# GpSimd's gathers in two graph aggregations: the wait before each step's eight gathers moves from the preceding step's gathers to those of the step two back

## The chip, the cores and the metric

One core of a Trainium2 chip runs the whole program. A core has TensorE (PE in the profile, its weight loads PEld), VectorE (DVE), ScalarE (ACT), GpSimd (POOL) and SyncE (SP), each with its own instruction stream, and 16 DMA engines. The engines meet only at semaphores. The metric is the device time in microseconds (us) of one execution. The kernel before has a median of 7060.26 us over 3 runs (7059.98 to 7061.63).

## The reference, cut to what matters

The program is a graph network of two layers on 6250 nodes with 256 features and 200000 edges `src` to `dst`. In each layer an attention aggregation over the edges is added to a dense branch, and a mixture of experts follows. The aggregation is the part that the change touches (layer 0, per head; layer 1 has the same form with 4 x 64 columns):

```
e   = leaky_relu(s[row, head] + d[col, head], 0.2)
ex  = exp(e - m[row])
den = segment_sum(ex, row, num_segments=N)
out = segment_sum((ex / den[row])[:, None] * hW[col], row, num_segments=N)
```

So for every edge a row of a table (`hW` and the scores `d`) is fetched by `col`, scaled by a weight, and summed into the row of the node that the edge belongs to.

## The kernel before, in words

`stage_sort` sorts the edges; they lie in 1616 tiles of 128 edges. `stage_aggregate` (called once for each layer by `aggregate_passes`) walks over them in 202 steps of 8 tiles (`KT`), four steps to a turn (`STEP_RING`). Layer 0 gathers rows of 68 numbers, layer 1 rows of 260. A step goes through the engines like this:

- ScalarE copies the 8 columns of indices of a step four ahead into `st_idx` (L904).
- GpSimd issues 8 indirect DMAs, one for each tile, that gather 128 rows of the table into one of the four slots of `got` (L876). This is `gather`, and its waits are what the change touches. It waits for the indices (`idx_staged`), from the second turn on for `scaled` up to the step four back (which last read the slot it now writes), and for `gathered` of the preceding step. `gathered[r]` counts the first seven gathers of a step; the eighth has a semaphore of its own, `last_in[r]`.
- SyncE loads the list of target rows, broadcast over the partitions, into `spread` (L893).
- VectorE makes a one-hot matrix `hot` (L975) and its transposed form `hot_t` in BF16 (L982). When both `gathered` and `last_in` of a step say that it has landed, it works out the exponents (L993 to L1004; L993 is the first instruction that stands behind that wait).
- ScalarE takes the exponentials (L909, L912), VectorE scales the gathered rows with them into `weighted` (L1016).
- TensorE gets the scores of a later step (L937) and sums `weighted` into blocks of 128 nodes with `hot` as the weights (L952), in a low and a high half; VectorE adds the sums to `acc` (L1024).

Each engine's order is written out by hand. In one step VectorE goes: scale step i, add the high half of step i-1, `hot` of step i+1, `hot_t` of step i+2, exponents of step i+1, add the low half of step i. Between these a "guest", the layer's dense branch, has its turn: `BallMix` in layer 0 (one tile of 128 nodes in four steps), `GateMix` in layer 1 (one tile in two steps, first "keys" in 100 steps, then "out"). The guests use TensorE, VectorE, ScalarE and SyncE, never GpSimd. TensorE's guest work stands between the scores and the high half of a step.

The DMAs of GpSimd elsewhere in the program (in the experts of layer 0, L1933 and L1939) have a wait and a `nop` ahead of each of them, but are written out without a loop.

The order in which GpSimd gathers: the first turn stands alone, then `Fori` loops over the turns, then the last turn.

Of the kernel before, what the change touches and what calls it, by code (L numbers as in the profile page):

```python
# [26 lines left out]
STEP_RING = 4  # L27
# [743 lines left out]
def stage_aggregate(nc, g, tag, table, width, shared, rows, row_list, acc, top, guest):  # L771
# [10 lines left out]
    with stage(nc) as own:  # L782
# [49 lines left out]
        def steps_of(last):  # L832
            return range(ENDING if last else STEP_RING)
# [30 lines left out]
        @block.gpsimd  # L864
        def _(pool):
            def gather(turn, r, first):
                j = turn * STEP_RING + r
                pool.wait_ge(idx_staged, j + 1)
                if not first:
                    pool.wait_ge(scaled, j - (STEP_RING - 1))  # L870
                if not first or r > 0:
                    t, q = (turn, r - 1) if r else (turn - 1, STEP_RING - 1)
                    pool.wait_ge(gathered[q], t * (16 * (KT - 1)) + 16 * (KT - 1))
                pool.nop(nofuse=True)
                for k in range(KT):
                    pool.indirect_dma_start(got[:, r, k, :], None, table,  # L876
                                            bass.IndirectOffsetOnAxis(ap=st_idx[:, r, k:k + 1], axis=0))\
                        .then_inc(gathered[r] if k < KT - 1 else last_in[r], 16)
            for r in range(STEP_RING):
                gather(0, r, True)  # L880
            with pool.Fori(1, TURNS - 1) as turn:
                for r in range(STEP_RING):
                    gather(turn, r, False)
            for r in steps_of(True):
                gather(TURNS - 1, r, False)
# [2287 lines left out]
```

## Time and profile before

| | us |
|---|---|
| median of 3 runs | 7060.26 |
| the profiled execution, its own time | 7063.9 |
| span of the profiled execution (first to last instruction) | 7062.1 |
| aggregation of layer 0, first gather to its end, from the span's start | 495 to 2741 |
| aggregation of layer 1, the same | 3581 to 5875 |
| busy over the span: PE, DVE, POOL, ACT | 5095.9, 4389.3, 3469.1, 1783.8 |
| mean granted TensorE clock, share of full speed | 0.83 |

The two aggregations are 4540 us of the span, nearly two thirds. A group of instructions in the profile is a line of the kernel, an engine, an operation and the buffers that it writes and reads, with its count, its busy time, the mean length of one in ns, and the idle time of the engine just ahead of it, by what ended that idle time ("issue": nothing that the profile shows). In a timeline each line starts with the start and the length in us, and ends with the idle time ahead of it in brackets. For a DMA that GpSimd issues the length is the time that the issuing takes; the data land later.

### The profile page before, as it was taken

How to read it: one execution, taken by the hardware profiler on the slowest of the kernel's cores; microseconds unless marked ns; L12 is line 12 of the kernel's file. 1: busy time of each engine (PE TensorE's matmuls, PEld its weight loads, DVE VectorE, ACT ScalarE, POOL GpSimd, SP SyncE). 2: the span in 40 equal slices, each digit the busy share in tenths (PEclk: the TensorE clock that was granted, in tenths of full speed). 3: DMA queues.
4: the chain of work that ended last, by engine and by line, in shares of the span. 5: the costliest groups of instructions: out<-in, count | busy, mean ns of one | idle time of the engine just before them, and what ended most of it. 6: DMA issues, size and time to landing. Idle time of an engine off the chain costs nothing. (4 is left out here: it accounts for less than half of the span.)

```text
span 7062.1 us, 90296 instructions
## 1 busy us (share of the span) xinstructions
PE 5095.9 (72%) x21196; PEld 3660.6 (52%) x21197; DVE 4389.3 (62%) x8953; ACT 1783.8 (25%) x4856; POOL 3469.1 (49%) x3669
## 2 busy tenths in 40 slices
PE   1446666666666664699766666667777777999999
PEld 1445555555555552466534444445555555666666
DVE  8987777777777778722566655556666667333333
ACT  7322222222222222222310000001111113433332
POOL 0126767666767766144146666666666664000000
PEclk8668888888888886799878887877777777999999
DMA  1022222222222222322444444444444444000001
GB/s 55 22 44 51 52 52 52 52 51 52 52 52 52 52 51 58 116 64 64 145 135 124 125 123 123 123 124 130 130 132 132 132 131 114 5 5 4 9 4 36
DMA packets 380644, 534.45 MB, mean 76 GB/s; under 512 B 119264, under 2 KB 240119, under 8 KB 380407
## 3 DMA queue, kind: packets, MB, share of 16 engines
q0 software_dynamic: 139648, 299.92, 17.8%
q1 hardware_dynamic: 240886, 233.29, 11.2%
q8 instruction: 43, 0.70, 0.0%
q14 instruction: 67, 0.54, 0.0%
HBM read 475.96 MB, written 56.96 MB: 75 GB/s over the span
## 5 line engine op out<-in xcount | busy, mean ns | idle before, releaser
L876 POOL DMA_INDIRECT got<-table,st_idx x3232 | 3092.9, 957 | 1453.5 <-issue 1004.8
L952 PE MATMUL ps_sum<-weighted,hot 128*128 128x260 f32 x6464 | 1861.2, 447 | 143.2 <-DVE acc L1024 139.0
L952 PEld LDWEIGHTS ps_sum<-weighted,hot 128*128 128x128 f32 x6464 | 1403.1, 229 | 563.0 <-DVE acc L1024 228.8
L1024 DVE TENSOR_TENSOR acc<-acc,ps_sum 128x260 f32 x1664 | 707.1, 425 | 890.3 <-PE ps_sum L952 750.0
L937 PE MATMUL ps_score<-score_split,hot_t 128*128 x3232 | 250.1, 188 | 1294.7 <-DVE z L1004 1267.5
L937 PEld LDWEIGHTS ps_score<-score_split,hot_t 128*128 128x128 bf16 x3232 | 196.8, 103 | 1471.7 <-issue 1456.7
L1016 DVE TENSOR_TENSOR weighted<-got,ps_weight 128x2048 f32<-128x2048 f32 x404 | 921.5, 2281 | 4.3 <-ACT weighted L912 0.8
L909 ACT ACTIVATE ps_weight<-z 128x32 f32<-128x32 f32 x404 | 81.2, 201 | 2969.8 <-DVE z L1004 2969.8
L3058 DVE SCALAR_TENSOR_TENSOR x_res<-ps_yf,comb,x_res 128x256 f32 x392 | 189.7, 484 | 638.0 <-PE ps_yf L2966 638.0
L975 DVE TENSOR_TENSOR hot<-ps_score,row_loc 128x1024 f32<-128x1024 f32 x404 | 492.1, 1218 | 3.5
L993 DVE TENSOR_REDUCE row_score<-ps_score 128x64 f32<-128x192 f32 (+1 forms) x404 | 163.3, 404 | 520.3 <-DMA got<-table,st_idx 518.9
L2946 PE MATMUL ps_hf<-acc,ws_f 128*128 (+2 forms) x896 | 348.2, 542 | 6.0 <-ACTq L2993 6.0
L2966 PE MATMUL ps_yf<-ws_f,h2t 128*128 128x256 f32 x1568 | 347.7, 379 | 0.8 <-ACT h2t L3006 0.8
L2946 PE MATMUL ps_hf<-h1t,ws_f 128*128 128x384 f32 (+1 forms) x896 | 346.0, 539 | 0.8 <-ACT h1t L3006 0.8
L2966 PEld LDWEIGHTS ps_yf<-ws_f,h2t 128*128 128x128 f32 x1568 | 297.8, 190 | 53.6 <-ACT h2t L3006 1.4
L3006 ACT ACTIVATE h2t<-ps_hf,own_scale 128x512 f32<-128x512 f32 x224 | 162.3, 725 | 507.9 <-PE ps_hf L2946 507.9
L2946 PEld LDWEIGHTS ps_hf<-acc,ws_f 128*128 128x128 f32 x896 | 171.1, 191 | 173.6 <-issue 114.8
L2946 PEld LDWEIGHTS ps_hf<-h1t,ws_f 128*128 128x128 f32 x896 | 170.2, 190 | 156.0 <-issue 107.1
L263 POOL TENSOR_TENSOR shifted<-xs,pivot 128x256 f32<-128x256 f32 x49 | 43.1, 880 | 382.4 <-DVE pivot L401 230.5
L1283 PE MATMUL ps_mix<-mix_xin,wq 128*128 128x128 f32 x1176 | 227.5, 379 | 0.4
L1283 PEld LDWEIGHTS ps_mix<-mix_xin,wq 128*128 128x128 f32 x1176 | 217.7, 289 | 3.7
L1939 POOL DMA_INDIRECT y_rows<-y_e,slot_home x108 | 106.6, 987 | 209.6 <-DVE y_e L2030 205.0
(533 smaller groups left out, 7558.3 us busy)
## 6 DMA issues: line engine op xcount, KB each, us to landing
spread<-row_list SPq DMA_DIRECT2D x404, 256.0 KB
got<-table,st_idx POOLq DMA_INDIRECT x3232, 2.8
gate_xin<-ball_rows SPq DMA_DIRECT2D x98, 128.0 KB
got_y_e<-y_rows SPq DMA_DIRECT2D x10, 896.0 KB
table<-row_e SPq DMA_DIRECT2D x50, 130.0 KB, 2.6
ball_rows<-xt SPq DMA_DIRECT2D x10, 640.0 KB, 4.7
mix_xin<-ball_rows SPq DMA_DIRECT2D x49, 128.0 KB
xn_rows<-xs_m SPq DMA_DIRECT2D x49, 128.0 KB, 1.7
```

Source lines behind the costliest of these rows:

```text
L876: pool.indirect_dma_start(got[:, r, k, :], None, table, bass.IndirectOffsetOnAxis(ap=st_idx[:, r, k:k + 1], axis=0))\
L937: last = nc.tensor.matmul(scores[:, k, :], hot_t[:, r % 2, k, :], split[:, :, :, :].rearrange("p t a c -> p (t a c)")[:, ds(b * SP, SP)], ...
L952: last = nc.tensor.matmul(ps_g[:, p % 2, 0:AW], hot[:, r % 2, k, :], weighted[:, r % 2, k, :], start=(k == n * p), stop=(k == n * p + n - 1))
L975: nc.vector.tensor_tensor(hot[:, r % 2, :, :], count_to.unsqueeze(1).to_broadcast([P, KT, P]), g.row_loc[:, ds(i * KT, KT)].unsqueeze(2).t ...
L993: link(nc.vector.tensor_reduce(row_score[:, :, :], scores.rearrange("p k (a c) -> p k c a", a=PARTS), AX.X, ALU.add))
L1016: nc.vector.tensor_tensor(out, v, w, ALU.mult).then_inc(scaled, 1)
L1024: nc.vector.tensor_tensor(acc[:, ds(b * AW, AW)], acc[:, ds(b * AW, AW)], ps_g[:, p % 2, 0:AW], ALU.add).then_inc(added, 1)
L1283: last = nc.tensor.matmul(bank[:, m * P:(m + 1) * P], self.mix.wq[:, c, (m0 + m) * P:(m0 + m + 1) * P], self.xin[:, c, :], start=(c == 0), ...
L2946: last = nc.tensor.matmul(ps_h[:, j, 0:HALVES[hf][1]], ws[:, par, l, c, f * P:(f + 1) * P], rhs(c, hf), start=(c == 0), stop=(c == 1))
L2966: last = nc.tensor.matmul(ps_y[:, k % 4, 0:D], h2[:, c, k * P:(k + 1) * P], ws[:, par, 2, c, :], start=(c == 0), stop=(c == 1))
L3006: nc.scalar.activation(h[:, f, at:at + n], ps_h[:, j, 0:n], ACT.Relu, bias=own_s[:, par, 1, l, f:f + 1], scale=own_s[:, par, 0, l, f:f + 1])\
L3058: nc.vector.scalar_tensor_tensor(xr, ps_y[:, k % 4, 0:D], comb[:, ds(t * 8 + pair * 2 + par, 1)], xr, ALU.mult, ALU.add).then_inc(y_used, 1)
```

## The change

In `gather`, the index of the awaited `gathered` semaphore goes from r-1 to r-2 of the ring of four (with the turn before where that is negative), and in the first turn step 1 has no such wait any more. All else is the same: the number of instructions on every engine but for that first-turn wait, the ring of four slots, the other two waits, what VectorE waits for before it reads a slot.

```
@@ -868,8 +868,8 @@
                 pool.wait_ge(idx_staged, j + 1)
                 if not first:
                     pool.wait_ge(scaled, j - (STEP_RING - 1))
-                if not first or r > 0:
-                    t, q = (turn, r - 1) if r else (turn - 1, STEP_RING - 1)
+                if not first or r > 1:
+                    t, q = (turn, r - 2) if r > 1 else (turn - 1, STEP_RING + r - 2)
                     pool.wait_ge(gathered[q], t * (16 * (KT - 1)) + 16 * (KT - 1))
                 pool.nop(nofuse=True)
                 for k in range(KT):
```

## Rows read from the trace of the kernel before

**Rows 1.** Stretches: layer 0, layer 1 keys, layer 1 out; busy us by engine.

```profile
core 0: us, PE busy (x) PEld busy (x) DVE busy (x) ACT busy (x) POOL busy (x), PEclk, DMA share, GB/s
495.00:2741.00 2246.00, 1501.48 (x7470) 1223.38 (x7470) 1648.96 (x2828) 594.55 (x2023) 1559.58 (x1616) 0.83 0.25 52
3581.00:4727.00 1146.00, 758.81 (x2904) 492.33 (x2904) 691.20 (x1321) 78.81 (x404) 768.90 (x810) 0.80 0.46 125
4727.00:5875.00 1148.00, 860.46 (x3156) 621.88 (x3156) 722.69 (x1431) 216.22 (x544) 764.42 (x806) 0.75 0.47 128
```

**Rows 2.** Timeline of POOL in layer 0, the end of one step and the next's start.

```profile
1808.63 1.21 POOL L876 DMA_INDIRECT got<-table,st_idx  x1 [0.30 <-issue]
1810.14 0.95 POOL L876 DMA_INDIRECT got<-table,st_idx  x1 [0.30 <-issue]
1812.23 0.94 POOL L876 DMA_INDIRECT got<-table,st_idx  x1 [1.14 <-DMA got<-table,st_idx]
1813.48 1.05 POOL L876 DMA_INDIRECT got<-table,st_idx  x1 [0.30 <-issue]
```

**Rows 3.** Timeline of POOL in layer 1, the first gather of a step.

```profile
4542.34 0.94 POOL L876 DMA_INDIRECT got<-table,st_idx  x1 [1.28 <-DMA got<-table,st_idx]
```

**Rows 4.** Line L876 in layer 0 (495 to 2741): us from issue to landing.

```profile
DMA to landing us min/median/max: 2.3/2.5/4.1
```

**Rows 5.** Line L876 in layer 1 (3581 to 5875): us from issue to landing.

```profile
DMA to landing us min/median/max: 2.7/2.8/4.7
```

**Rows 6.** Groups by line, POOL, layer 0 (495 to 2741).

```profile
L876 POOL DMA_INDIRECT got<-table,st_idx x1616 | 1559.6, 965 | 694.8 <-issue 494.8 <-DMA got<-table,st_idx 165.5 <-DVE weighted L1016 17.4
```

**Rows 7.** The same, layer 1 keys (3581 to 4727).

```profile
L876 POOL DMA_INDIRECT got<-table,st_idx x810 | 768.9, 949 | 388.6 <-issue 255.9 <-DMA got<-table,st_idx 117.5 <-ACT st_idx L904 14.5
```

**Rows 8.** The same, layer 1 out (4727 to 5875).

```profile
L876 POOL DMA_INDIRECT got<-table,st_idx x806 | 764.4, 948 | 370.2 <-issue 254.0 <-DMA got<-table,st_idx 115.6 <-ACT st_idx L904 0.6
```

**Rows 9.** Timeline of POOL: the stages' first gathers, a first and a last stall.

```profile
495.42 1.44 POOL L876 DMA_INDIRECT got<-table,st_idx  x1 [16.38 <-ACT st_idx L904]
...
653.26 0.95 POOL L876 DMA_INDIRECT got<-table,st_idx  x1 [1.68 <-issue]
...
3581.77 1.19 POOL L876 DMA_INDIRECT got<-table,st_idx  x1 [12.35 <-ACT st_idx L904]
...
5853.10 0.94 POOL L876 DMA_INDIRECT got<-table,st_idx  x1 [1.67 <-issue]
```

**Rows 10.** Waits of POOL over the span, for the gathers of the experts: total, times, longest.

```profile
POOL xin_e L1933 <- issue: 31.7, 104, 0.3
```

**Rows 11.** Timeline of POOL: the shortest idle time ahead of a step.

```profile
2134.30 0.94 POOL L876 DMA_INDIRECT got<-table,st_idx  x1 [0.72 <-DMA got<-table,st_idx]
```

**Rows 12.** Timeline, all engines: the scaling of one step, and the slot's next gather.

```profile
1826.42 2.28 DVE L1016 TENSOR_TENSOR weighted<-got,ps_weight 128x2048 f32<-128x2048 f32 x1
...
1829.69 0.22 ACT L904 COPY st_idx<-col_idx 128x8 int32 x1
...
1855.69 0.94 POOL L876 DMA_INDIRECT got<-table,st_idx  x1 [1.15 <-DMA got<-table,st_idx]
```

**Rows 13.** Groups by line, DVE, layer 0 (495 to 2741).

```profile
L1024 DVE TENSOR_TENSOR acc<-acc,ps_sum 128x260 f32 x819 | 347.9, 425 | 265.3 <-PE ps_sum L952 190.6 <-DVE acc L1024 57.6
L982 DVE TENSOR_SCALAR hot_t<-spread,lane 128x1024 bf16<-128x1024 bf16 x202 | 101.6, 503 | 0.1
L993 DVE TENSOR_REDUCE row_score<-ps_score 128x64 f32<-128x192 f32 x202 | 71.7, 355 | 297.4 <-DMA got<-table,st_idx 296.9
```

**Rows 14.** Groups by line, DVE, layer 1 keys (3581 to 4727).

```profile
L1024 DVE TENSOR_TENSOR acc<-acc,ps_sum 128x260 f32 x397 | 168.7, 425 | 279.3 <-PE ps_sum L952 244.5 <-DVE acc L1024 26.3
L993 DVE TENSOR_REDUCE row_score<-ps_score 128x96 f32<-128x288 f32 x101 | 45.9, 455 | 150.9 <-DMA got<-table,st_idx 150.8
```

**Rows 15.** Groups by line, DVE, layer 1 out (4727 to 5875).

```profile
L1024 DVE TENSOR_TENSOR acc<-acc,ps_sum 128x260 f32 x423 | 179.9, 425 | 337.8 <-PE ps_sum L952 307.6 <-DVE acc L1024 22.4
L993 DVE TENSOR_REDUCE row_score<-ps_score 128x96 f32<-128x288 f32 x101 | 45.7, 452 | 72.0 <-DMA got<-table,st_idx 71.2
```

**Rows 16.** Timeline of DVE: one `hot_t`, beside the gather at 1813.48.

```profile
1813.24 0.48 DVE L982 TENSOR_SCALAR hot_t<-spread,lane 128x1024 bf16<-128x1024 bf16 x1
```

More of the change, by code:

```diff
@@ L870, in gather @@
                     pool.wait_ge(scaled, j - (STEP_RING - 1))
-                if not first or r > 0:
-                    t, q = (turn, r - 1) if r else (turn - 1, STEP_RING - 1)
+                if not first or r > 1:
+                    t, q = (turn, r - 2) if r > 1 else (turn - 1, STEP_RING + r - 2)
                     pool.wait_ge(gathered[q], t * (16 * (KT - 1)) + 16 * (KT - 1))
```

## The prediction

> **What bounds the kernel now.** First look at the stretches, since the two aggregations differ from the rest and from each other [rows 1]. No engine is busy for more than three quarters of any of the three stretches: in layer 0 VectorE 1649 of 2246 us, GpSimd 1560; in layer 1 GpSimd 769 and 764, TensorE 759 and 860, VectorE 691 and 723. Busy shares name no bound, so the next view is GpSimd's timeline. There the starts of gathers inside a step stand 1.25 us apart (0.94 of issuing, 0.30 of idle time called issue), whatever the other engines do, and only ahead of a step's first gather is there a hole: 1.14 us in layer 0, 1.28 in layer 1 [rows 2, 3], put down to the gathers themselves. The landing times say why. From the start of the seventh gather, issue alone would reach the next step after two gathers and two gaps, 2 x (0.94 + 0.30) = 2.5 us; the seventh lands at a median 2.5 us in layer 0 and 2.8 in layer 1 [rows 4, 5], and the release takes some time on top. So GpSimd waits for its own last transfers at every step, and starts the next step late.
>
> Does anyone wait for GpSimd? VectorE's first instruction behind the gathers, L993, stood idle for them for 296.9 us in layer 0, 150.8 in the keys and 71.2 in the out stretch [rows 13 to 15]. So in all three GpSimd's pace is VectorE's pace for much of the time: 2246, 1146 and 1148 us over 202, about 101 and about 101 steps are 11.1, 11.3 and 11.4 us each, and eight gathers with their hole make up the same.
>
> **The change, part by part.** It adds no instruction and no wait, removes one wait in the first turn, and makes the awaited semaphore one that is older by a step. The gathers awaited then were issued some 11 us earlier and have landed within 4.7 us at most [rows 4, 5]: the wait is always met. What is late next: the other two waits. The scaling that frees a slot ended at 1828.70 and the indices were copied by 1829.91, while the gather that needs both started at 1855.69 [rows 12]; over 25 us of room, so neither takes over before GpSimd has run some two steps further ahead. Nothing else moves: no DMA is issued in another order on POOL's queue or SP's, only earlier. `spread` keeps its own pace from `hot_t`.
>
> **The hole, added up.** All idle time ahead of L876, less what stays. Layer 0: 694.8 us [rows 6], less 16.4 for the first gather, less 1615 x 0.30 = 484.5 for plain issue, less 18 stalls of 1.68 (one every 88 gathers, the second of a step, in both layers; they lie inside a step and stay) at 1.38 over issue = 24.8 [rows 9]: 169 us over 201 step borders. Keys: 388.6 [rows 7] - 12.4 - 809 x 0.30 - 8 x 1.38 = 122. Out: 370.2 [rows 8] - 806 x 0.30 - 10 x 1.38 = 115. So 406 us are what GpSimd would save if a border cost no more than plain issue.
>
> What will a border cost? Not shown, as each one now waits. From below: the gathers of the experts have a met wait and a `nop` ahead of each, and 104 of them took 31.7 us of idle time, 0.30 each [rows 10]. But those waits are written out; here the awaited counts come out of a loop's register. From above: the shortest border now has 0.72 with the wait in it [rows 11]. I take 0.40, nearer to the first, since GpSimd can work out a count while the last gather is being issued. That gives back 0.10 x 402 borders: 149, 112 and 105 us.
>
> **What VectorE lets through.** It can't gain more than it now waits. Layer 0: 296.9 against 149, all of it passes. Keys: 150.8 against 112, passes. Out: 71.2 against 105, so 71 pass, and from there VectorE and TensorE set the pace (VectorE waits 307.6 us for TensorE's sums there [rows 15]). The four slots even out the long and short steps of the guests, with 25 us of room, but not perfectly where the two paces are close: I take off 15 us, a tenth of layer 1's 183, an estimate. Sum: 149 + 112 + 71 - 15 = 317 us. Against the profiled execution's own 7063.9 us that is 6747; the median of the runs is 3.6 lower, so **6743**, as a round figure 6745.
>
> A gather that is issued in the hole's old place can also collide with VectorE. `hot_t` at 1813.24 ran beside a gather of 1.05 us [rows 2, 16], 0.11 over the usual, while `hot_t` itself takes 503 ns in the mean against 478 in that row [rows 13]. GpSimd issues for 1560 of layer 0's 2246 us [rows 1], so about two in three already run beside a gather; if all the others now cost 0.11, it would be 404 x 0.31 x 0.11 = 14 us. The pause is only a part of the rest, so I put it at nothing and leave the 14 us to the range.
>
> The Trainium skill speaks against the change here: SBUF — State Buffer, section "SBUF: two separate sides", says that GpSimd cannot write DMA descriptors while VectorE runs in a two-port performance mode, and is blocked until that ends. By that rule each `hot_t` would hold up a gather for up to its whole 0.48 us, up to 97 us a layer if all were new. The trace has 0.11 in this row instead, and the collisions are mostly there already.
>
> **The rivals.** *VectorE and TensorE take it back.* VectorE's waits for gathers may have covered other work, so that waits for TensorE's sums, 244.5 and 307.6 us in layer 1 already [rows 14, 15], grow by what those shrink. For it: in layer 1 a step's guest stands on TensorE ahead of the high half, at a granted clock of 0.80 and 0.75 [rows 1]. Against it: TensorE's scores wait for the exponents, so that most of this order moves along with the gathers. If all of layer 1 falls away, 149 stay: 6911. Its extreme is that nothing passes in layer 0 either: 7060.
>
> The Trainium skill would have it so: Perfetto Trace Analysis, section "Identifying the Most-Contended Engine", takes the engine of highest occupancy as the bottleneck, and for GpSimd occupancy as a fair measure. By that rule VectorE binds layer 0 and TensorE the out stretch. The trace disagrees as far as VectorE's 296.9 us of idle time go.
>
> *The border costs far more than issue.* If the three waits on register counts take a full 1.0 us, 0.70 over issue on 402 borders, 281 of the 406 us stay: 6935. Against it: at 0.72 there is already a border that includes a wait for data.
>
> *Slower: without the pause, issuing stretches.* The wait lets the transfers drain once a step. Without it two or three gathers are in flight all the time, and if each then takes longer to issue, eight of them count at every step. The price: the gather of 1.21 us at 1808.63 [rows 2], 0.27 over 0.94, at all eight is 2.2 us a step, 870 us over 404 steps; less the 406, 464 are lost: 7525. It decides from 406 / 3232 = 0.13 us longer for each gather. Against it: inside a step gathers already follow each other at 1.25 us with two in flight, from the second to the eighth, without getting longer, and the DMA engines are busy for only 0.25 and 0.46 of these stretches [rows 1].
>
> **Chances.** My forecast 0.74; VectorE and TensorE take back layer 1's part 0.12, all of it 0.03; a costly border 0.06; slower 0.05. The forecast's own range goes from 406 us saved (borders at 0.30, and an out stretch that speeds up all the way), 6655, to borders at 0.72, 0.42 x 402 = 169 us back, with 71 at most in the out stretch: 85 + 79 + 71 = 235 saved, less the 15: 6840. To hold 8 in 10 the range must reach the first rival's 6911: 6665 to 6915, the lowest 10 us left out as two favourable ends together. Faster by over 0.2% (14 us, about what a measurement of this kernel can tell from no change) 0.92, within it 0.03, slower 0.05.
>
> **What would show it.** Right: the idle time ahead of a step's first gather is 0.30 to 0.45 us; GpSimd's idle time in layer 0 falls from 695 to about 550; its length of a gather stays at 0.94 to 0.97; VectorE's wait for gathers halves in layer 0 and nearly vanishes in the out stretch, where GpSimd starts to wait for the scaling (L1016) of the step four back; the layers take some 2100 and 2125 us in place of 2246 and 2294. Wrong: a hole of 0.7 us or more that nothing in the profile explains; VectorE's wait on TensorE's sums longer by what it no longer waits for gathers; gathers of over 1.08 us in the mean.

## The result, and the profile after

The changed kernel takes **6631.35 us** in the median of 4 runs (6630.09 to 6632.97), the kernel before 7060.53 in 4 runs beside it: a ratio of 0.9392, with an interval of 0.9376 to 0.9408. That is 429 us saved. The forecast was 317, and its range ended at 6665: the direction and the place were right, the size was too small. The profiled run after took 6631.9 us, with a span of 6630.1; the span before was 7062.1. So 432.0 us are to be accounted for.

First the kernel's stretches after, by windows (the columns are those of [rows 1]: length, busy us of TensorE, its weight loads, VectorE, ScalarE and GpSimd, then granted clock, DMA share, GB/s). They are cut at round numbers and hold about 201, 100 and 101 steps:

```profile
494.00:2540.00 2046.00, 1421.12 (x7461) 1136.64 (x7462) 1635.02 (x2817) 594.18 (x2021) 1544.67 (x1616) 0.87 0.26 57
3384.00:4400.00 1016.00, 728.68 (x2895) 484.88 (x2896) 689.32 (x1312) 78.18 (x398) 769.35 (x808) 0.83 0.51 139
4400.00:5430.00 1030.00, 808.41 (x3144) 585.55 (x3143) 713.41 (x1423) 215.59 (x545) 770.47 (x809) 0.78 0.52 144
```

All three are 9 to 11% shorter, GpSimd's busy time in each is what it was within 1%, and TensorE's granted clock is higher (0.83, 0.80 and 0.75 before). Now GpSimd's timeline in layer 0, with two step borders that the trace marks (start, length, then in brackets the idle time ahead and its releaser):

```profile
1652.67 1.31 POOL L876 DMA_INDIRECT got<-table,st_idx  x1 [0.30 <-issue]
1654.28 0.95 POOL L876 DMA_INDIRECT got<-table,st_idx  x1 [0.30 <-DMA got<-table,st_idx]
1655.54 0.95 POOL L876 DMA_INDIRECT got<-table,st_idx  x1 [0.31 <-issue]
```

The hole of 1.14 us [rows 2] is 0.30 here, like any gap inside a step. All 402 borders are 0.30 or 0.31. And of the 36 stalls of 1.68 us [rows 9] none is left: no gap inside a step is above 0.32. GpSimd's group of gathers in the three stretches (count, busy us, mean ns, idle time and its releasers), to be held against [rows 6 to 8]:

```profile
L876 POOL DMA_INDIRECT got<-table,st_idx x1616 | 1544.7, 956 | 507.6 <-issue 444.6 <-DMA got<-table,st_idx 46.6 <-ACT st_idx L904 16.3
L876 POOL DMA_INDIRECT got<-table,st_idx x808 | 769.8, 953 | 258.4 <-issue 236.9 <-ACT st_idx L904 12.3 <-DMA got<-table,st_idx 7.6
L876 POOL DMA_INDIRECT got<-table,st_idx x809 | 771.0, 953 | 246.7 <-issue 235.4 <-DMA got<-table,st_idx 10.4 <-ACT st_idx L904 0.6
```

The 46.6 us that are still put down to gathers are no wait for data: they are 153 gaps of 0.30 or 0.31 us, as long as the gaps put down to issue. Last, VectorE's two waits, stretch by stretch, against [rows 13 to 15]:

```profile
L1024 DVE TENSOR_TENSOR acc<-acc,ps_sum 128x260 f32 x814 | 345.6, 425 | 202.5 <-PE ps_sum L952 131.9 <-DVE acc L1024 53.0
L993 DVE TENSOR_REDUCE row_score<-ps_score 128x64 f32<-128x192 f32 x201 | 71.0, 353 | 174.0 <-DMA got<-table,st_idx 173.3
L1024 DVE TENSOR_TENSOR acc<-acc,ps_sum 128x260 f32 x396 | 168.3, 425 | 245.0 <-PE ps_sum L952 211.3 <-DVE acc L1024 25.3
L993 DVE TENSOR_REDUCE row_score<-ps_score 128x96 f32<-128x288 f32 x100 | 45.3, 453 | 60.2 <-DMA got<-table,st_idx 60.2
L1024 DVE TENSOR_TENSOR acc<-acc,ps_sum 128x260 f32 x416 | 176.9, 425 | 291.2 <-PE ps_sum L952 261.3 <-DVE acc L1024 22.2
L993 DVE TENSOR_REDUCE row_score<-ps_score 128x96 f32<-128x288 f32 x101 | 45.3, 449 | 7.0 <-DMA got<-table,st_idx 7.0
```

The wait for gathers shrinks in each stretch (296.9, 150.8 and 71.2 before), as forecast. What was not forecast: the wait for TensorE's sums shrinks as well (190.6, 244.5 and 307.6 before).

**Where the 432 us come from.** GpSimd's run of gathers went from 2238.0 to 2037.1 us in layer 0 and from 2279.8 to 2032.3 in layer 1, so 200.8 and 247.4 less. The borders' idle time alone, summed over 201 borders each, fell from 222.9 to 61.3 and from 291.3 to 61.3: 392 together. The 36 stalls gave 49 us, and the gathers themselves, with their plain gaps, are 8 us in all shorter. Against these stand 16 us outside: VectorE, which follows GpSimd, is further behind when GpSimd's last gather is done, so the stretch from layer 0's last gather to layer 1's first grew by 4.5 us, the part behind layer 1 by 12.6, while the start is 0.9 shorter. By steps, counted on VectorE from one scaling (L1016) to the next:

| us per step: whole / wait for sums / wait for gathers / rest | layer 0 | keys | out |
|---|---|---|---|
| before | 11.08 / 0.95 / 1.48 / 8.66 | 11.23 / 2.44 / 1.51 / 7.28 | 11.36 / 3.04 / 0.70 / 7.61 |
| after | 10.12 / 0.66 / 0.86 / 8.59 | 10.00 / 2.11 / 0.61 / 7.28 | 10.25 / 2.63 / 0.06 / 7.55 |

In the out stretch each step is 1.11 us shorter, though VectorE had only 0.70 us of waiting for gathers to give: 0.64 came from there, 0.41 from the wait for TensorE's sums and 0.06 from the rest. That is the miss to be explained.

### The profile page after: what moved, and what is told of

It reads as the page before. It is cut to its first block and busy times, and to the rows that moved or that the text cites. A ratio compares the mean times of both kernels' runs of the same rounds, so it can differ in the third digit from the quotient of the medians.

```text
span 6630.1 us, 90296 instructions
## 1 busy us (share of the span) xinstructions
PE 4948.0 (75%) x21196; PEld 3538.8 (53%) x21197; DVE 4374.5 (66%) x8953; ACT 1782.7 (27%) x4856; POOL 3464.2 (52%) x3669
## 5 line engine op out<-in xcount | busy, mean ns | idle before, releaser
L876 POOL DMA_INDIRECT got<-table,st_idx x3232 | 3084.5, 954 | 1012.4 <-issue 916.7
L952 PEld LDWEIGHTS ps_sum<-weighted,hot 128*128 128x128 f32 x6464 | 1387.5, 226 | 589.3 <-DVE acc L1024 257.7
L1016 DVE TENSOR_TENSOR weighted<-got,ps_weight 128x2048 f32<-128x2048 f32 x404 | 921.5, 2281 | 4.3 <-ACT weighted L912 0.8
L3006 ACT ACTIVATE h1t<-ps_hf,own_scale 128x512 f32<-128x512 f32 x224 | 162.2, 724 | 173.5 <-PE ps_hf L2946 173.5
L1968 PE MATMUL ps_he<-w1s,xt_e 128*128 x432 | 204.4, 596 | 0.1
```

The source lines that it names most:

```text
L876: pool.indirect_dma_start(got[:, r, k, :], None, table, bass.IndirectOffsetOnAxis(ap=st_idx[:, r, k:k + 1], axis=0))\
L952: last = nc.tensor.matmul(ps_g[:, p % 2, 0:AW], hot[:, r % 2, k, :], weighted[:, r % 2, k, :], start=(k == n * p), stop=(k == n * p + n - 1))
L1016: nc.vector.tensor_tensor(out, v, w, ALU.mult).then_inc(scaled, 1)
L1968: last = nc.tensor.matmul(ps_h[:, r % 2, :], xt[:, r % 2, c, :], inputs.w1s[:, :, :].rearrange("p a n -> p (a n)")[:, ds(e * (2 * WIDE_E) ...
L3006: nc.scalar.activation(h[:, f, at:at + n], ps_h[:, j, 0:n], ACT.Relu, bias=own_s[:, par, 1, l, f:f + 1], scale=own_s[:, par, 0, l, f:f + 1])\
```

## The experiments

They ran in three groups, each on a chip of its own beside the kernel before (which took 7050.05 us beside the first four, 7052.13 beside the next four, and 7052.3 in the median of 9 beside the last two). Each time is that of one run, but for the last two kernels with five runs each. "Per step" is always counted as in the table above. The first question is what a border costs and where the stalls went, the second why VectorE waits less for TensorE.

### No wait for gathers at all

```diff
 (from the changed kernel)
-                if not first or r > 1:
-                    t, q = (turn, r - 2) if r > 1 else (turn - 1, STEP_RING + r - 2)
-                    pool.wait_ge(gathered[q], t * (16 * (KT - 1)) + 16 * (KT - 1))
```

> The wait of GpSimd for its own gathers is taken out altogether; the waits for indices and for scaled slots stay. Theory R (only the landing of the awaited gather costs, and once it is met early nothing is left to gain): the same as the changed kernel, 6631 us within 10, 0.30 us ahead of every step, no idle time over 0.35 inside a step. Rival Q (the wait also keeps the queue of transfers short, and the step two back is still part of that): gathers get longer than 0.96 us in the mean and the time is over 6650.

Measured: 6637.66 us. All 402 borders 0.30 or 0.31, a gather 953 ns in the mean, GpSimd's runs 2035.5 and 2028.5 us, against 2037.1 and 2032.3 with the wait (the 6 us to 6631 are within what five runs of the changed kernel differ by, below). The whole group on the page:

```profile
L876 POOL DMA_INDIRECT got<-table,st_idx x3232 | 3084.5, 954 | 1012.4 <-issue 916.7
```

is that of the changed kernel; without the wait the idle time is 1012.4 as well:

```profile
L873 POOL DMA_INDIRECT got<-table,st_idx x3232 | 3078.9, 953 | 1012.4 <-issue 973.5 <-ACT st_idx L901 32.9 <-DVE weighted L1013 6.1
```

So a wait that is already met when GpSimd comes to it costs nothing that the trace can show, and the change has taken out all there was to take out at the border. One stall is left, against what was expected, in the last step of layer 1:

```profile
5403.22 0.94 POOL L873 DMA_INDIRECT got<-table,st_idx  x1 [1.26 <-issue]
```

There the scaling that frees the slot had ended only 1.16 us before the step's first gather started; this stall comes back below. That gathers would hold each other up without the pause (Q) falls with the same line: they are no longer than before (957 ns over both layers).

### The preceding step's first six, and first four

The wait goes back to the preceding step, but to fewer of its gathers: the first six (a landing 1.25 us earlier than the seventh's) or the first four (3.75 us earlier).

```diff
 (from the changed kernel; first four: 4 and 4 in place of 6 and 2)
-                if not first or r > 1:
-                    t, q = (turn, r - 2) if r > 1 else (turn - 1, STEP_RING + r - 2)
-                    pool.wait_ge(gathered[q], t * (16 * (KT - 1)) + 16 * (KT - 1))
+                if not first or r > 0:
+                    t, q = (turn, r - 1) if r else (turn - 1, STEP_RING - 1)
+                    pool.wait_ge(gathered[q], t * (16 * 6) + 16 * 6)
...
-                        .then_inc(gathered[r] if k < KT - 1 else last_in[r], 16)
+                        .then_inc(gathered[r] if k < 6 else last_in[r], 16)
...
-                dve.wait_ge(gathered[r], turn * (16 * (KT - 1)) + 16 * (KT - 1))
-                dve.wait_ge(last_in[r], turn * 16 + 16)
+                dve.wait_ge(gathered[r], turn * (16 * 6) + 16 * 6)
+                dve.wait_ge(last_in[r], turn * (16 * 2) + 16 * 2)
```

> As before, but GpSimd waits for the first six gathers of the preceding step, not seven (the two others share the second semaphore). Theory R: the sixth starts 3.74 us ahead of the moment at which the next step could be issued; it lands after 2.5 us in layer 0 and 2.8 in layer 1, and 0.7 us go from landing to the next start, 3.2 and 3.5: met in time, 0.30 ahead of nearly every step in layer 0 and 0.30 to 0.45 in layer 1, and a time of 6631 to 6700, where the upper end is with the 36 stalls of 1.68 us back. Rival D (any wait for the preceding step drains GpSimd's instructions and costs, whichever gather it names): 0.5 us or more ahead of each step, over 6710.

> The same with the first four gathers of the preceding step. Theory R: met 3 us ahead of time, 0.30 everywhere, and the stalls of 1.68 us hidden as in the changed kernel, 6631 within 10. If the stalls need the step two back, 36 x 1.38 = 50 us more, 6681. Rival D: over 6700.

Measured: 6671.29 us with six, 6625.89 with four. With six, 200 of layer 0's 201 borders are at 0.30, and 161 of layer 1's (the others reach up to 2.08, mean 0.40). And all 36 stalls are back, in their old places, but shorter, all but four in layer 1: 0.84 to 1.26 us in layer 0, 1.17 to 1.68 in layer 1. The first one of each layer, from GpSimd's timeline of that kernel:

```profile
637.48 0.99 POOL L876 DMA_INDIRECT got<-table,st_idx  x1 [1.19 <-issue]
...
3543.46 0.94 POOL L876 DMA_INDIRECT got<-table,st_idx  x1 [1.48 <-issue]
```

With four, all borders are at 0.30, layer 0 has no stall and layer 1 two short ones (0.69 and 0.87). The sizes fit together. Before, the median hole was 1.03 us in layer 0 and 1.36 in layer 1, 0.73 and 1.06 more than a border that need not wait. The sixth gather is issued 1.25 us ahead of the seventh, so the wait is now met 0.52 and 0.19 us before GpSimd comes to it; the median stalls (1.09 and 1.45) are 0.59 and 0.23 shorter than 1.68. With four it is met some 2.7 us early or more, and the stall's 1.38 us are gone but for the two. So the stall is not time that must pass between two gathers: it behaves like work ahead of the issuing, covered as far as GpSimd has its wait behind it early. The one stall without any such wait, above, fits: it stands where another wait, the one for the scaling, was met only about a microsecond early. The forecast's step two back isn't needed for either gain, only a wait that is met early. That the border would keep a cost of its own (D) falls.

### All eight gathers of the preceding step

```diff
 (from the kernel before)
                     pool.wait_ge(gathered[q], t * (16 * (KT - 1)) + 16 * (KT - 1))
+                    pool.wait_ge(last_in[q], t * 16 + 16)
```

> As before, with a second wait: for the eighth gather of the preceding step too. Theory R: the hole grows by one gather with its gap, 1.25 us, at 402 borders, 503 us: 7560, with 2.3 and 2.7 us ahead of each step. Theory C (TensorE's granted clock falls when it idles longer, and its guest matmuls and so VectorE's wait for sums get longer): granted clock below 0.83 in layer 0 and below 0.78 over layer 1, VectorE's wait for TensorE's sums above 190.6 us in layer 0 and above 552 in layer 1. Rival T (the sums are waited for less in the changed kernel because of the order of things, not the clock): that wait and the lengths of TensorE's guest matmuls as before, within 5%.

Measured: 7655.21 us, 605 over the kernel before (95 more than the 7560 expected). A border of layer 0 in its timeline, and the group of VectorE's waits over the whole span:

```profile
1510.85 0.94 POOL L877 DMA_INDIRECT got<-table,st_idx  x1 [2.21 <-DMA got<-table,st_idx]
```

```profile
L1025 DVE TENSOR_TENSOR acc<-acc,ps_sum 128x260 f32 x1664 | 707.3, 425 | 937.9 <-PE ps_sum L953 802.1 <-DVE acc L1025 102.8
L994 DVE TENSOR_REDUCE row_score<-ps_score 128x64 f32<-128x192 f32 (+1 forms) x404 | 164.3, 407 | 1062.8 <-DMA got<-table,st_idx 1062.4
```

One transfer more to wait for makes the holes 2.80 us in the mean of layer 0 and 2.78 in that of layer 1. They were 1.11 and 1.45, and one more issue of 1.25 would make 2.36 and 2.70. So layer 1 is nearly as expected, and layer 0 is not: half of its holes lie at 2.1 to 2.5, many others at 3.1 to 3.8, as if the eighth transfer often landed later after its issue than the seventh did. Why, wasn't looked into. For the second question the other number counts: VectorE now waits **longer** for TensorE's sums, 802.1 us against 750.0 before, with the same work on TensorE, and the granted clock is lower, 0.80, 0.77 and 0.74. That is the reverse of what the change did. Most of it is in layer 0 (0.95 to 1.12 us a step); over layer 1 the wait is only 3% longer, which theory T, with its 5%, would allow as well.

### Idle work on TensorE, at the old pace

Here nothing changes for GpSimd. In layer 0 and in the keys, but not in the out stretch, TensorE gets four BF16 matmuls a step whose result nobody reads, in the time in which it would wait for the scores' turn.

```diff
 (from the kernel before)
+        ps_fill = own.enter_context(nc.psum_tensor("ps_fill" + tag, [P, 512], F32)) if shared else None
...
                 pe.wait_ge(hot_t_ready, i + 1)
+                to = ps_fill[:, :] if shared else guest.banks[:, 3, :]
+                if not (first and r < 2) and (shared or guest.phase in ("first", "keys")):
+                    for _ in range(4):
+                        nc.tensor.matmul(to, g.ident_h[:, :], split[:, :, :, :].rearrange("p t a c -> p (t a c)")[:, 0:512], start=True, stop=True)
```

> The kernel before with four idle matmuls (128 x 512, BF16, into PSUM that nobody reads) on TensorE ahead of its wait for the exponents, in layer 0 and in the keys of layer 1, none in the out stretch. They shorten TensorE's idle time, and leave GpSimd's gathers as late as before. Theory C (the longer idle time lowers TensorE's granted clock; that made the guests' matmuls slow and VectorE wait for sums): granted clock in layer 0 from 0.83 to 0.87 or more and in the keys from 0.80 to 0.83 or more, the guest matmuls of layer 0 (weights wq) from 379 to under 345 ns, VectorE's wait for sums in layer 0 below 170 us from 190.6, and its wait for gathers longer by as much; the out stretch as before. The time as before within 15 us, since GpSimd paces it. Rival T (the gathers' earlier landing itself shortens the wait for sums): clock and guest matmuls as before, the wait for sums as before or longer by the idle matmuls.

Measured: 7061.57 us. The same windows as [rows 1], then VectorE's two waits in layer 0 and in the keys:

```profile
495.00:2741.00 2246.00, 1658.88 (x8283) 1239.18 (x8284) 1648.70 (x2836) 593.76 (x2023) 1555.91 (x1616) 0.86 0.24 52
3581.00:4727.00 1146.00, 823.56 (x3274) 500.49 (x3274) 685.28 (x1307) 78.11 (x398) 760.85 (x803) 0.84 0.45 122
4727.00:5875.00 1148.00, 863.57 (x3164) 623.07 (x3164) 724.78 (x1436) 216.45 (x547) 765.86 (x808) 0.75 0.46 129
```

```profile
L1029 DVE TENSOR_TENSOR acc<-acc,ps_sum 128x260 f32 x826 | 350.6, 424 | 243.9 <-PE ps_sum L957 169.1 <-DVE acc L1029 57.6 <-issue 0.2
L998 DVE TENSOR_REDUCE row_score<-ps_score 128x64 f32<-128x192 f32 x202 | 71.8, 356 | 319.0 <-DMA got<-table,st_idx 318.6
L1029 DVE TENSOR_TENSOR acc<-acc,ps_sum 128x260 f32 x396 | 168.2, 425 | 246.9 <-PE ps_sum L957 209.5 <-DVE acc L1029 28.9
L998 DVE TENSOR_REDUCE row_score<-ps_score 128x96 f32<-128x288 f32 x101 | 46.0, 455 | 193.2 <-DMA got<-table,st_idx 193.2
```

With more work on TensorE its clock is higher where it got the work (0.83 to 0.86, 0.80 to 0.84; out stays at 0.75), and VectorE waits less for its sums: 169 us against 191 in layer 0, 210 against 245 in the keys. The guest's matmuls of layer 0 (the same line is L1283 before and L1288 here) are shorter too:

```profile
L1283 PE MATMUL ps_mix<-mix_xin,wq 128*128 128x128 f32 x1176 | 227.5, 379 | 0.4
L1288 PE MATMUL ps_mix<-mix_xin,wq 128*128 128x128 f32 x1176 | 202.7, 349 | 0.5
```

Two of C's figures are missed narrowly: 349 ns for under 345, and a clock of 0.86 in layer 0 for 0.87 or more. So the clock moves the waits by itself, with GpSimd as it was; T, by which clock and wait should have stayed, falls. The move is as large as the change's own in the keys (2.44 to 2.10 us a step, 2.11 after the change), and less than half of it in layer 0 (0.95 to 0.83, 0.66 after the change). And the time doesn't fall, since GpSimd sets the pace: what VectorE no longer waits for sums, it waits for gathers (318.6 for 296.9, 193.2 for 150.8). A shorter wait for sums is worth something only once GpSimd no longer waits for itself.

### Two kernels with idle instructions on GpSimd

The stalls come at the 114th gather of a layer and then every 88. Is it a count of instructions? One kernel puts one `nop` more ahead of each gather of the kernel before, the other 16 into each border of the changed one.

```diff
 (from the kernel before)
                 for k in range(KT):
+                    pool.nop(nofuse=True)
                     pool.indirect_dma_start(got[:, r, k, :], None, table,
```

```diff
 (from the changed kernel)
                 j = turn * STEP_RING + r
+                for _ in range(16):
+                    pool.nop(nofuse=True)
                 pool.wait_ge(idx_staged, j + 1)
```

> The changed kernel with 16 no-operations of GpSimd at each border, ahead of the three waits. Theory R (GpSimd's waits and register work are done while the gathers before are still being issued, so a met border costs no more than plain issue): 0.30 us ahead of each step, 6631 within 12. Rival B (work at the border is added to it, and the border was just cheap): 16 x 0.03 to 0.06 us = 0.5 to 1.0 more at 402 borders, 6830 to 7030.

Measured: 7053.5 us, against 7052.13 for the kernel before, with the stalls where they were; and 6630.29 us with borders of 0.30 and no stall. Neither says anything: the traces list 90296 instructions in the first, as many as in the kernel before, and 98 more than after in the second, where thousands were added. Whether the idle instructions ran at all can't be seen, so the question goes to the next run. Nor does any run show what a no-operation costs: the 0.03 to 0.06 us of the two expectations stay without one.

### Half of the gathers

Only the first four of a step's eight gathers are issued; the other half of each slot is set to zero once. So this kernel leaves out half of the gathered rows, and its time is no time for the whole work. It shows the pace that is left when GpSimd is no limit.

```diff
 (from the changed kernel)
-                    pool.wait_ge(gathered[q], t * (16 * (KT - 1)) + 16 * (KT - 1))
+                    pool.wait_ge(gathered[q], t * (16 * 3) + 16 * 3)
...
-                for k in range(KT):
+                for k in range(4):
...
-                        .then_inc(gathered[r] if k < KT - 1 else last_in[r], 16)
+                        .then_inc(gathered[r] if k < 3 else last_in[r], 16)
...
+            nc.vector.memset(got[:, :, 4:KT, :], 0.0).then_inc(cleared, 1)
```

> The changed kernel with only four of each step's eight gathers; the other half of each slot is set to zero once, so half of the edges carry no data. GpSimd needs 5 us for a step, and VectorE and TensorE set the pace alone. Prediction's step (VectorE can't gain more than it waited for gathers, the rest stays): 2246 - 297 = 1949 us for layer 0, 995 and 1077 for the keys and out stretches, 4021 together. Theory C (the rest shrinks too, as TensorE idles less and its clock stays up): layer 0 below 1880, keys below 960, out below 1025, with a granted clock over 0.87, 0.83 and 0.78.

Measured: 6241.57 us; layer 0 in 1793, the keys in 855 and the out stretch in 1026 us (one more than the 1025 expected). The groups on GpSimd and VectorE, and a stall in GpSimd's timeline:

```profile
L876 POOL DMA_INDIRECT got<-table,st_idx x1616 | 1530.8, 947 | 2139.5 <-DVE weighted L1016 1278.9 <-ACT st_idx L904 465.7 <-issue 394.3
```

```profile
L1024 DVE TENSOR_TENSOR acc<-acc,ps_sum 128x260 f32 x1664 | 706.8, 425 | 619.4 <-PE ps_sum L952 477.8 <-DVE acc L1024 107.7 <-issue 0.4
L993 DVE TENSOR_REDUCE row_score<-ps_score 128x64 f32<-128x192 f32 (+1 forms) x404 | 161.2, 399 | 0.0
```

```profile
727.98 0.95 POOL L876 DMA_INDIRECT got<-table,st_idx  x1 [1.96 <-issue]
```

VectorE never waits for a gather, GpSimd waits for slots (the scaling, 1278.9 us), and the wait for sums is 477.8 us, 272 less than before. If VectorE could gain no more than its own waits for gathers, layer 0 would take 1931 us, the keys 972 and the out stretch 1076 (2228, 1123 and 1148 before, counted from scaling to scaling like the measured times, less 297, 151 and 71; the expectation's 1949, 995 and 1077 count from first gathers). They take 1793, 855 and 1026, at granted clocks of 0.93, 0.90 and 0.78, the last one not over 0.78 as expected. The out stretch takes hardly less than after the change (10.16 us a step, against 10.25): there VectorE and TensorE set the pace once the holes are gone. This kernel also gathers half the bytes, so by itself it doesn't tell the clock from a lighter load on the DMA engines.

The stalls are back here, as GpSimd waits again, and they are longer, 1.95 to 2.06 us. The first is again at the 114th gather, though that is now the 29th step and not the 15th, and then they come every 100 gathers (25 steps of four) in place of 88 (11 steps of eight). The first place speaks for a count of gathers (G). The spacing fits neither theory as it was put: G has every 88, and by F more instructions per gather mean fewer gathers between two stalls, not more. In both kernels a stall stands only at the second gather of a step, right behind a wait; if there were others in places where they are covered, the rows wouldn't show them. So what is counted, and what GpSimd does then, stays open.

### The changed kernel again, and idle work in its out stretch

If the clock holds the out stretch back after the change, then idle work there must gain time, where it gained none before. In every second step of the out stretch TensorE gets four idle matmuls, into a bank that is free by then.

```diff
 (from the changed kernel)
                 pe.wait_ge(hot_t_ready, i + 1)
+                if not (first and r < 2):
+                    guest.warm(pe, turn, r, split[:, :, :, :].rearrange("p t a c -> p (t a c)")[:, 0:512])
...
+    def warm(self, pe, turn, r, operand):
+        turn, r = (turn, r - 2) if r >= 2 else (turn - 1, r + 2)
+        if self.phase == "out" and r % 2 == 1:
+            pe.wait_ge(self.mixed, self.out_tile(turn, r, 1))
+            for _ in range(4):
+                self.nc.tensor.matmul(self.banks[:, 3, :], self.g.ident_h[:, :], operand, start=True, stop=True)
```

> The changed kernel itself, as the measure for the next run: 6631 us within 10 by every theory, since nothing in it differs.

> The changed kernel with four idle matmuls (128 x 512, BF16, into the PSUM bank of the guest's projection while nobody uses it) on TensorE ahead of its wait for the exponents, in every second step of the out stretch: the only stretch that VectorE and TensorE pace in the changed kernel (10.25 us a step, where GpSimd could do 10.03). Theory C: the granted clock there from 0.78 to 0.82 or more, VectorE's wait for sums from 2.63 us a step to under 2.4, the stretch 10 to 20 us shorter, 6610 to 6622. Rival T: the idle matmuls only delay the scores; the same time or up to 20 us more.

Measured, five rounds on one chip: the changed kernel 6620.54 us (6618.52 to 6631.69), ratio 0.9391 (0.9378 to 0.9404), just outside the 6631 within 10 that was expected; with idle work 6612.94 (6610.53 to 6614.46), ratio 0.9376 (0.9363 to 0.9389). That is 7.6 us by the medians. The intervals of the ratios overlap, but each of the five runs is below each of the other five. The out stretch in both, by the same window, first without, then with the idle work:

```profile
4400.00:5417.00 1017.00, 802.40 (x3102) 583.11 (x3103) 702.35 (x1403) 214.73 (x542) 765.70 (x807) 0.78 0.53 146
```

```profile
4400.00:5417.00 1017.00, 794.83 (x3329) 562.37 (x3330) 718.05 (x1422) 214.67 (x545) 763.86 (x806) 0.83 0.53 145
```

TensorE has 227 matmuls more in this window, 184 of them idle ones (the rest is work that comes earlier), and is busy 8 us less, at 0.83 for 0.78. VectorE's two waits there, in the same order:

```profile
L1024 DVE TENSOR_TENSOR acc<-acc,ps_sum 128x260 f32 x407 | 173.1, 425 | 290.5 <-PE ps_sum L952 260.9 <-DVE acc L1024 22.0
L993 DVE TENSOR_REDUCE row_score<-ps_score 128x96 f32<-128x288 f32 x100 | 44.9, 449 | 7.6 <-DMA got<-table,st_idx 7.5
```

```profile
L1026 DVE TENSOR_TENSOR acc<-acc,ps_sum 128x260 f32 x416 | 176.9, 425 | 240.8 <-PE ps_sum L954 210.9 <-DVE acc L1026 22.2
L995 DVE TENSOR_REDUCE row_score<-ps_score 128x96 f32<-128x288 f32 x101 | 45.6, 452 | 41.5 <-DMA got<-table,st_idx 41.2
```

Counted by steps, VectorE's wait for sums falls from 2.64 to 2.11 us a step, its wait for gathers rises from 0.06 to 0.40, and the step is 10.11 us for 10.26: 15 us over 101 steps, which is most of what the profiled runs differ by (17 us). The profiled run of the changed kernel is the slowest of its five, so the 7.6 us of the medians are the better measure of the gain. T, by which the idle matmuls would only delay the scores, falls here.

## Why the prediction was right or wrong, point by point

**What bounds the kernel: right.** GpSimd's wait for its own last transfers set the pace of all three stretches. Taking it away made every stretch shorter, and making it longer by one transfer made every stretch longer.

**"The hole, added up": right**, 406 us forecast, of which the borders gave 392 when they fell to plain issue. The 14 us between are mostly rounding: a plain gap is 0.305 us, and the sum took it as 0.30 some 3200 times.

**"What will a border cost?": too dear.** I took 0.40 and measured 0.30 at all borders, the lower bound from [rows 10]. The awaited count out of a loop's register costs nothing beside the issue of the gather ahead. With 402 borders that is 40 us of the miss.

**"They lie inside a step and stay": wrong.** All 36 stalls went, 49 us, the largest single term that the sum left out. The kernel with the first six gathers awaited shows when they go: a stall is covered as far as GpSimd's wait is met early. What a stall is stays open.

**"It can't gain more than it now waits": the step that failed in its logic.** I capped the out stretch at VectorE's 71 us of waiting for gathers, and took 15 us off layer 1 for an imperfect fit; 34 and 15 us of the miss. The cap took the wait for TensorE's sums as given. It wasn't: of the 1.11 us that a step of the out stretch lost, 0.41 came from that wait. It goes with TensorE's granted clock, here over the kernels of this document (granted clock, then VectorE's wait for sums in us a step, from scaling to scaling):

| clock / wait for sums | layer 0 | keys | out |
|---|---|---|---|
| all eight gathers awaited | 0.80 / 1.12 | 0.77 / 2.60 | 0.74 / 3.08 |
| before | 0.83 / 0.95 | 0.80 / 2.44 | 0.75 / 3.04 |
| before, idle work in layer 0 and keys | 0.86 / 0.83 | 0.84 / 2.10 | 0.75 / 3.03 |
| after | 0.88 / 0.66 | 0.83 / 2.11 | 0.78 / 2.63 |
| after, half of the gathers | 0.93 / 0.36 | 0.90 / 1.39 | 0.78 / 2.59 |
| after, idle work in the out stretch | 0.88 / 0.66 | 0.85 / 2.00 | 0.83 / 2.11 |

Two rows tell the clock from the landing of the gathers. In the out stretch half of the gathers, never waited for, leave clock and wait nearly as they are after the change. And idle work, which brings no gather earlier, raises the clock and shortens the wait. Only in layer 0 it shortens the wait by less than the change did, and how much of the rest is the clock's isn't shown.

Why was the clock lower before? The rows of single steps show it, by windows of 1 us (columns as in [rows 1]) and by the first matmul behind a pause. Before, in the out stretch, TensorE did nothing from 5218.3 to 5223.0; within that pause its clock fell from 1.00 to 0.50, that is from 2.4 to 1.2 GHz, and it stayed there until 5232.7, for over 9 us of full work:

```profile
5219.00:5220.00 1.00, 0.00 (x0) 0.00 (x0) 0.00 (x0) 0.00 (x0) 0.47 (x1) 1.00 0.37 108
...
5223.00:5224.00 1.00, 0.97 (x9) 0.91 (x10) 0.73 (x2) 0.98 (x3) 0.71 (x1) 0.50 0.29 54
5231.00:5232.00 1.00, 1.00 (x4) 0.81 (x3) 0.40 (x2) 0.00 (x0) 0.24 (x1) 0.50 0.55 133
```

```profile
5223.03 0.62 PE L937 MATMUL ps_score<-score_split,hot_t 128*128 x8 [4.75 <-DVE z L1004]
```

After, in one such place, the pause is 2.26 us and the clock stays up:

```profile
4861.00:4862.00 1.00, 0.00 (x0) 0.00 (x0) 0.87 (x5) 0.00 (x0) 0.70 (x2) 1.00 0.54 183
...
4864.00:4865.00 1.00, 1.00 (x6) 0.89 (x5) 1.00 (x1) 0.28 (x2) 0.87 (x1) 1.00 0.94 338
```

```profile
4850.43 0.60 PE L937 MATMUL ps_score<-score_split,hot_t 128*128 x8 [1.96 <-DVE z L1004]
...
4862.45 0.59 PE L937 MATMUL ps_score<-score_split,hot_t 128*128 x8 [2.26 <-DVE z L1004]
```

Single pauses don't settle it: behind the shorter pause of 1.96 us the clock of that kernel does fall, from 4852 to 4858. The whole out stretch shows more. TensorE has 101 pauses of over 1 us there in either kernel, 286 us in sum before and 216 after. Of those over 4 us there are 15 before and none after, and in or within 1.5 us behind each of the 15 the clock fell; of the shorter ones it fell at 60 of 86 before and at 48 of 101 after. The time at 1.2 GHz went from 584 us in 88 pieces to 454 in 81.

So VectorE can gain more than it waited for gathers: the pauses on TensorE get shorter, what follows them runs more often at the upper clock, and the sums come earlier. The Trainium skill describes this in TensorE: Matmul & The Clock Gate, section "HAM oscillation — how this bites in real kernels", with a kernel in which TensorE is throttled again at each wait for a transfer; the trace agrees, with the 0.50 above, though here only some of the shorter pauses had a fall behind them.

**What the sum left out: the ends.** 16 us were lost as VectorE trails GpSimd further at the end of each layer.

The terms of the miss together, in us:

| term | forecast | measured |
|---|---|---|
| borders | 406 - 40 = 366 | 391.6 |
| cap in the out stretch, imperfect fit | -34 - 15 | 0 |
| stalls | 0 | 48.9 |
| length of the gathers and their plain gaps | 0 | 7.7 |
| around the layers | 0 | -16.2 |
| sum | 317 | 432.0 |

**The range** left the best 10 us out "as two favourable ends together". Both came, and the stalls with them: 406 us saved would have been 6655, and the result is 24 below even that.

**The rivals.** *VectorE and TensorE take it back* fell: each stretch's wait for sums is shorter. *The border costs far more than issue* fell at 0.30. *Slower, since issuing stretches* needed gathers longer by 0.13 us; they are 0.009 shorter in layer 0 (965 to 956 ns) and 0.004 longer in layer 1's (949 and 948 to 953). What was to show it right has one miss: in the out stretch GpSimd didn't come to wait for the scaling. No such wait is in its rows; its lead over VectorE, from the first gather to the scaling of a layer's last step but one, grew from 18 to 22 us in layer 0 and from 22 to 32 in layer 1, still within the four slots.

**The two rules of the Trainium skill.** By the lock that the Trainium skill gives in SBUF — State Buffer, section "SBUF: two separate sides", more gathers beside `hot_t` should have cost time. More of them do run beside one (192 before and 270 after in layer 0, 198 and 231 in layer 1), but they cost next to nothing: after the change such a gather takes 954 ns in layer 0 against 956 for the others, and 977 against 949 in layer 1. By the Trainium skill's Perfetto Trace Analysis, section "Identifying the Most-Contended Engine", VectorE would have bound layer 0 before, at 1649 of 2246 us [rows 1]; the stretch took 200 us less with VectorE's work unchanged. For the out stretch the prediction read that page too widely: the page calls TensorE's busy time no good measure and judges that engine by the arithmetic done or by its weight loads, 622 us there [rows 1], so that by weight loads it names GpSimd, at 764 us, and not TensorE.

## What to carry to other kernels

Read the bound from the spacing of an engine's instructions and from who ended its idle time, not from busy shares; then price a wait that will be met at plain issue, and also what recurring stalls it will cover. A cap on the gain of "what the next engine waits for me now" is too low where that engine also waits for TensorE, and TensorE idles long enough to lose its clock: look at the granted clock of each stretch and at TensorE's pauses in it, and give shorter pauses a gain of their own. Where TensorE's clock is what binds, idle matmuls in its pauses can pay (7.6 us here); where another engine sets the pace, they only move a wait.

## What the runs showed that was not expected

- An indirect gather of 128 rows on GpSimd costs 0.95 + 0.30 us with no wait for earlier ones as well: the mean was 953 ns then, with two or three in flight by the landing times of 2.5 and 2.8 us.
- GpSimd takes 1.38 us extra at a layer's 114th gather and then every 88 (with four gathers to a step every 100, and 1.65 us or more). With the wait met some 2.7 us early or more, 34 of 36 are hidden and the other two are shorter. What it is, and what it counts, stays open.
- More work on TensorE made TensorE's busy time shorter: with 184 idle matmuls more in the out stretch it was busy 8 us less, at a granted clock of 0.83 for 0.78.
- The kernel that waits for a step's last gather as well lost 605 us. In layer 0 that is 1.69 us a border in place of the 1.25 that one more issue takes, with two groups of holes (2.1 to 2.5 and 3.1 to 3.8). This wasn't followed up.
